# Attention in a fused convolution block: the finished output of a superblock is copied out of the matmul bank by the vector engine instead of ScalarE

## What is computed

```python
x = x + _L0_conv_ref(_gn(x), ...)   # filters that depend on pixel and channel
x = x + _L1_conv_ref(_gn(x), ...)   # a gate from a mean key
x = x + _L2_conv_ref(_gn(x), ...)   # 3x3 convolution with ternary weights
x = x + _L3_conv_ref(_gn(x), ...)

def _L3_conv_ref(x, q_w, k_w, v_w):
    xf = x.reshape(b, din, hw)
    Q = jnp.einsum('kc,bcp->bkp', q_w, xf)
    K = jnp.einsum('kc,bcp->bkp', k_w, xf)
    V = jnp.einsum('vc,bcp->bvp', v_w, xf)
    S = jnp.einsum('bkp,bkq->bpq', Q, K)
    A = jax.nn.softmax(S, axis=-1)
    z = jnp.einsum('bpq,bvq->bvp', A, V)
```

## Time and profile before

| | |
|---|---|
| median of 3 runs | 1719.05 us (1707.12 to 1719.12) |
| the profiled execution, own time | 1707.5 us |
| its span, first to last instruction | 1705.7 us |
| PE busy | 1604.1 us (94%) |
| PE weight loads (overlap PE) | 862.6 us (51%) |
| DVE busy | 1214.4 us (71%) |
| ACT busy | 1192.2 us (70%) |
| POOL busy | 1112.8 us (65%) |
| mean granted clock of PE | 0.956 |

### The profile page before, as it was taken

The page is one execution under the profiler, slowest core; times in us unless marked ns, Lnnn a source line. Parts: engine busy times, 40 slices in busy tenths (PEclk is TensorE's granted clock), DMA queues, the critical chain, the costliest instruction groups (busy, mean ns, idle before and its releaser), DMA issues.

```text
span 1705.7 us, 29329 instructions
## 1 busy us (share of the span) xinstructions
PE 1604.1 (94%) x10783; PEld 862.6 (51%) x10783; DVE 1214.4 (71%) x2330; ACT 1192.2 (70%) x2268; POOL 1112.8 (65%) x886
## 2 busy tenths in 40 slices
PE   5989979979988899999999999999999999999996
PEld 4457438438446334555555555555555555555542
DVE  5855864765664877777777777777777777777760
ACT  2053133224322679999999999999999999999984
POOL 1720540360261258888888888888888888888887
PEclk9988988998899699999999999999999999999998
DMA  2000210210304500500000500000140000000000
GB/s 94 5 34 38 68 38 38 67 38 1 105 1 62 177 1 7 108 18 12 12 12 12 91 34 12 12 12 18 27 93 12 12 13 18 12 7 7 7 7 11
DMA packets 15584, 57.64 MB, mean 34 GB/s; under 512 B 4688, under 2 KB 10960, under 8 KB 13008
## 3 DMA queue, kind: packets, MB, share of 16 engines
q1 hardware_dynamic: 15440, 55.77, 12.2%
HBM read 31.41 MB, written 24.22 MB: 33 GB/s over the span
## 4 chain that ended last, share of the span: by engine, by line
PE 83%; DVE 9%; POOL 4%; issue 2%; ACT 2%; DMA 0%; POOLq 0%; DVEq 0%; ACTq 0%
PE PS L1395 29%; PE PS L1330 15%; PE PS L1368 14%; PE PS L1279 6%; PE PS L1233 5%; PE PS L1221 3%; DVE nmt L749 2%; PE PS L1188 2%; PE PS L1318 2%; PE PS L1310 2%; POOL accP L1134 1%; PE PS L1268 1%; PE PS L1269 1%; DVE nmt L756 1%; DVE st L506 1%
## 5 line engine op out<-in xcount | busy, mean ns | idle before, releaser
L749 DVE TENSOR_REDUCE nmt<-PS 128x1 f32<-128x448 f32 x1323 | 767.3, 617 | 222.8 <-PE PS L1330 222.2
L1134 POOL TENSOR_TENSOR accP<-accP,Pb 128x512 f32<-128x512 f32 (+1 forms) x532 | 675.2, 1269 | 93.3 <-ACT Pb L1004 37.7
L1004 ACT ACTIVATE Pb<-PS 128x896 f32<-128x896 f32 (+1 forms) x700 | 636.9, 915 | 80.0 <-PE PS L1368 69.6
L969 ACT ACTIVATE PS<-PS,nmt 128x448 f32<-128x448 f32 x588 | 356.4, 606 | 17.6 <-DVE nmt L756 10.8
L1395 PE MATMUL PS<-Pb,VT 128*64 128x448 f32 x1400 | 336.0, 541 | 1.8 <-ACT Pb L1004 1.2
L1395 PE MATMUL PS<-Pb,xnf 128*64 128x448 f32 x1400 | 336.4, 540 | 0.0
L1330 PE MATMUL PS<-xnp,xin 96*64 96x448 bf16 x1408 | 265.5, 371 | 8.0 <-ACT PS L969 3.2
L1330 PE MATMUL PS<-Ka,Qa 96*64 96x448 bf16 x1372 | 258.8, 353 | 0.9
L1368 PE MATMUL PS<-xin,xnp 99*64 99x448 bf16 x1372 | 256.2, 353 | 0.8 <-ACT Pb L1004 0.6
L1368 PE MATMUL PS<-Qa,Ka 99*64 99x448 bf16 x1372 | 251.8, 353 | 0.0
L1330 PEld LDWEIGHTS PS<-xnp,xin 96*64 96x64 bf16 x1408 | 87.6, 113 | 138.9 <-issue 62.3
(11 more groups left out here) (159 smaller groups left out, 1820.7 us busy)
## 6 DMA issues: line engine op xcount, KB each, us to landing
saved_v<-VT SPq DMA_DIRECT2D x4, 1600.0 KB, 11.3
xin<-in_x SPq DMA_DIRECT2D x4, 1568.0 KB, 6.3
saved_x<-xw SPq DMA_DIRECT2D x4, 1568.0 KB, 5.2
out<-xw SPq DMA_DIRECT2D x28, 224.0 KB, 1.9
saved_parts<-parts SPq DMA_DIRECT2D x4, 1176.0 KB, 8.0
xw<-saved_x SPq DMA_DIRECT2D x21, 224.0 KB, 2.6
xnf<-saved_v SPq DMA_DIRECT2D x2, 1600.0 KB, 16.7
VT<-saved_v SPq DMA_DIRECT2D x2, 1600.0 KB, 17.9
```

What stands on the lines that cost most here:

```text
L749: nc.vector.reduce_max(nmt[:, target % 2, b, t:t + 1], PS[0:BLK, bank, 0:CH], X, negate=True).then_inc(mx_free, 1)
L969: return nc.scalar.activation(PS[0:BLK, bank, 0:CH], PS[0:BLK, bank, 0:CH], ACT.Exp, bias=nmt[:, target % 2, b, t:t + 1], accum_out=sm[:, ...
L1004: nc.scalar.activation(Pb[0:r, j % PSLOTS, :, :], PS[0:r, 2 * (k % 2):2 * (k % 2) + 2, 0:CH], ACT.Exp).then_inc(exp_done, 1)
L1134: nc.gpsimd.tensor_tensor((accQ if j < TO_ACCP else accP)[0:r, :, REST:CH], (accQ if j <= TO_ACCP else accP)[0:r, :, REST:CH], Pb[0:r, j % ...
```

## The change

The function `copy_output` goes from ACT's list to DVE's, with the same two waits and the same semaphore. On ACT it stood behind the exponential of step 0; on DVE it stands at the beginning of step 0, ahead of the maxima of that step's tiles. DVE's instruction is `tensor_copy`, in the place of an activation with the function Copy. PE, POOL and SP are the same.

```diff
@@ DVE, attention()
+                def copy_output(sidx):
+                    dve.wait_ge(pv_done, NQ * (sidx + 1) + PSLOTS)
+                    dve.wait_ge(fin_done, sidx + 1)
+                    nc.vector.tensor_copy(Osb[:, :], PS[:, OB, 0:CH]).then_inc(ocopy, 1)
+
                 def superblock(sidx):
...
                     for j in range(NQ):
+                        if j == 0 and sidx:
+                            copy_output(sidx - 1)
                         if j == FINISH_STEP and sidx:
                             turn_denominators(sidx - 1, DEN_BANK[sidx - 1][0] if sidx < SBS - 1 else 7)
...
                 for sidx in range(SBS):
                     superblock(sidx)
+                copy_output(SBS - 1)
                 turn_denominators(SBS - 1, 7)
@@ ACT, attention()
-                def copy_output(sidx):
-                    act.wait_ge(pv_done, NQ * (sidx + 1) + PSLOTS)
-                    act.wait_ge(fin_done, sidx + 1)
-                    nc.scalar.activation(Osb[:, :], PS[:, OB, 0:CH], ACT.Copy).then_inc(ocopy, 1)
-
...
                                              ACT.Exp).then_inc(exp_done, 1)
-                        if j == 0 and sidx:
-                            copy_output(sidx - 1)
                         if j in FACTOR_STEPS:
...
                 for sidx in range(SBS):
                     superblock(sidx)
-                copy_output(SBS - 1)
```

## The result

The changed kernel takes 1738.99 us (median of 4 runs, 1738.42 to 1739.61); the forecast was 1738.7. The kernel before took 1713.47 us in the four runs beside it, a ratio of 1.015 with a 95% interval of 1.0101 to 1.0199: slower, by less than 2%. The kernel before has a median of 1708.3 us in 25 later runs; against these the loss is 30.7 us, beside the 31.2 forecast.

A forecast was written before the change was run, and what follows sets the result against it. PE was taken to bound the kernel, waiting 1.2 us for each of 26 late DVE copies: 31.2 us on the profiled 1707.5 us gives 1738.7 us, 1.8% slower. The range was 1727 to 1755 us.

The forecast's parts named there:

- PE sets the period, ACT and DVE wait for it: In the attention, PE was to set the 38.85 us superblock period; DVE idles 8.1 us and ACT 2.3 us for PE.
- The forecast for ACT's idle time, 3.9 us: ACT's idle time per period was to grow to about 3.9 us (2.3 + 0.44 + 1.2).
- The copy starts 1.08 us after the first maximum: On DVE, the copy was to wait behind two maxima of step 24: 962.64 + 2 x 0.54 = 963.72.
- The copy takes 0.61 us: DVE's copy of 128x448 out of a bank: 0.61 us, from two other copy shapes; bounds 0.54 and 0.68.
- 1.2 us a copy, 26 times: Step 0's value matmuls on PE were to start 1.2 us late behind each of 26 copies: 31.2 us.
- The two terms of 0.05 us: First matmul behind a wait adds 0.05 us; the same 0.05 goes where step 1's exponential is no longer waited for.
- The bounds of 1.12 and 1.34: Loss per copy: 1.12 us with a copy of 0.54, 1.34 with one of 0.68 begun after the second maximum ended.
- The end hides the last two: Last two copies: DVE free, at most 0.1 us longer, hidden by PE's 4.68 us wait for POOL; cost zero.
- ACT's relief: Rival: ACT sets the pace and wins 0.44 us 27 times, 11.9 us, giving 1695.6 us; 4%.
- The wait was seen in full: Rival denied here: step 0's values would not wait for the copy, leaving 1707.5 us; 7%.
- none of the 1.2 us came back elsewhere: Rival denied here: PE's waits for DVE's maxima swallow part; half of it leaves 15.6 us, 1723.1 us; 8%.
- The granted clock did not fall: Rival denied here: PE's stop of about 1.0 us per period drops the clock, 44 us more, 1783 us; 5%.

The follow-up runs named there:

- copy_before_maxima: Against the changed kernel: DVE's copy moved one place earlier, ahead of the two maxima of step 24; 1708.33 us, ratio 1.0002.
- early_copy_turn_in_halves: Against the kernel before: copy on DVE ahead of step 24's maxima, DVE's turning back of denominators split over steps 4 and 5; 1700.94 us, ratio 0.9948.
- copy_between_maxima: Against the changed kernel: DVE's copy moved between the two maxima of step 24; 1726.52 us, ratio 1.0109.
- half_by_each: Against the changed kernel: ScalarE copies columns 224 to 447 at its old place, DVE only the left 224; 1733.04 us, ratio 1.0152.
- no_tiles_at_step_24: Against the changed kernel: the plan gives step 24 no tiles of maxima and two other steps a third; 1742.95 us, ratio 1.0202.

## Why the prediction was right

- **PE sets the period, ACT and DVE wait for it.** Held. ACT was relieved of its copy in copy_before_maxima and early_copy_turn_in_halves and the period stayed as it was with the copy on ScalarE (38.85, and 38.62). The forecast for ACT's idle time, 3.9 us, is 2.3 + 1.6 in the rows; but what ACT waits for behind the late values is not the scores of step 3, as the prediction says, but DVE's maximum of a tile that PE makes behind them.
- **The copy starts 1.08 us after the first maximum.** 1.07 measured. copy_between_maxima shows what one maximum ahead of the copy is worth: 0.53 us of the period. With both gone, in copy_before_maxima, the whole loss is gone.
- **The copy takes 0.61 us.** 0.614. The slope of 1.05 ns an element from two other shapes of a DVE copy out of a bank carried it; half_by_each shows it again, 234 ns for 224 elements.
- **1.2 us a copy, 26 times.** 1.23, and 26 waits. The handover takes 0.05 us (973.92 to 973.97), and the values start 1.18 us late, both as set down. The two terms of 0.05 us that were to cancel behind that start leave 0.05 us in the period; which of them was off was not separated. The bounds of 1.12 and 1.34 come out as 1.11 and 1.33 by the terms given for them. The tiles of the last superblock begin in step 18 of superblock 25 and not in step 0 of 26; the count of 26 stands.
- **The end hides the last two.** PE's last wait for POOL is 4.67 us, before 4.68:

```profile
1729.69 1.12 PE L1382 MATMUL PS<-accP,ones 128*64 128x256 f32 x4 [4.67 <-POOL accP L1134]
```

- **The rivals.** ACT's relief brought nothing. The wait was seen in full, and none of the 1.2 us came back elsewhere: PE's weight loads waited 1.9 us a period for maxima before and 1.7 now, and step 5 takes its 1.78 us in both. The granted clock did not fall between 650 and 1690 us.
- **What was off, and luck.** The forecast of 1.8% starts from the 1707.5 us of the profiled execution, the measured 1.5% from a median of 1713.47 us. The range's upper end allowed for runs 11.6 us above the profile; none of the four lay there. That the times agree to 0.3 us is partly luck: the four runs spread over 1.2 us, and the periods put the loss at 32.0 us, not 31.2.

## What to carry to other kernels

Ask where a moved instruction stands in the new engine's list and what that engine waits for there, before asking how busy it is: an engine with 8 us free of 39 made the bound engine late by 1.2 us, since the work ahead of the copy needed data made after the copy's own. If a wait must move to another engine, put it at the point where its data is there and the queue is empty; here that was two instructions earlier. And an engine with the larger load is not the bound while its idle time ends with another's result: relieving it was worth nothing, with the stop of step 5 and without it.

## What the runs showed of the hardware

The layers ahead of the attention did not take the same time in every traced execution, though the edits leave them alone. In no_tiles_at_step_24 the attention begins with the exponential at 616.82 us, in the kernel before with that at 605.66; two traces lie between (609.78 in copy_before_maxima, 610.62 in half_by_each). From 100 to 600 us the granted clock is 0.85 in the first and 0.87 in the kernel before, so more of that time lies at the 1.2 GHz level in the first. Why one execution has more of it stays open.

Busy times of no_tiles_at_step_24 in that stretch, then ACT's timeline:

```profile
100.00:600.00 500.00, 445.85 (x1795) 281.74 (x1793) 316.45 (x569) 164.72 (x275) 151.19 (x100) 0.85 0.17 50
```

```profile
616.82 0.92 ACT L1007 ACTIVATE Pb<-PS 128x896 f32<-128x896 f32 x1 [0.67 <-PE PS L1368]
```

The kernel before, the same two views:

```profile
100.00:600.00 500.00, 443.22 (x1837) 274.52 (x1837) 327.43 (x590) 170.96 (x292) 151.56 (x101) 0.87 0.18 54
```

```profile
605.66 1.73 ACT L1004 ACTIVATE Pb<-PS 128x896 f32<-128x896 f32 x2 [0.66 <-PE PS L1368]
```

A stop of PE of 1.02 us in every 40 us left the clock at 1.00 in the changed kernel from 650 to 1690 us. In the kernel before, the stop of 1.89 us in the first layer was followed by 0.51; no run here has a stop over 1.02 us between 650 and 1660 us. In the layers ahead of the attention stops also stand closer together: in the kernel before, one of 0.99 us begins 1 us behind one of 1.76, and soon after comes a stretch at 0.50. Whether length or spacing decides is not shown. PE's timeline there, and the busy times of that stretch:

```profile
227.52 0.38 PE L1169 MATMUL PS<-mv,cs 128*128 128x2 f32 x2 [1.76 <-DVE mv L511]
...
229.52 0.20 PE L1255 MATMUL PS<-pooled,wz 128*16 128x1 f32 x2 [0.99 <-DVE pooled L646]
...
230.94:234.35 3.41, 3.38 (x6) 1.51 (x5) 0.29 (x2) 1.21 (x2) 0.00 (x0) 0.50 0.00 0
```
